# Two cross-attentions of a perceiver: value products ahead of the next value projection, and the V copies behind three row maxima

## The chip, the cores and the metric

The kernel runs on one core of one Trainium2 chip. The metric is the time of a whole execution on the device in microseconds (us); lower is better. Engines are named as in the profile: PE is TensorE (PEld are its weight loads), DVE is VectorE, ACT is ScalarE, POOL is GpSimd and SP issues transfers.

## The reference

Six sublayers are added one after the other to a stream x of 16 sequences of 64 tokens and 256 features. Two of them, the first and the fourth, are cross-attentions to one context of 1601 rows for each sequence, with 16 heads of 16 features:

```
x = x + L0_xattn(layernorm(x), ctx)          # q k v, relative positions, softmax, Wo
x = x + L0_attn(layernorm(x))                # causal, latent keys and values
x = x + L0_ffn(layernorm(x))                 # 8 experts, top 2, and a shared one
x = x + L1_xattn(layernorm(x), ctx, mask)
x = x + L1_attn(layernorm(x))                # gated delta rule and a feed forward
x = x + L1_ffn(layernorm(x))                 # fp4 weights and activations

scores = einsum('bhid,bhjd->bhij', q, k) * scale
out    = einsum('bhij,bhjd->bhid', softmax(scores), v)
```

The first cross-attention also has a table of relative positions (`rel` in the code), the second a mask (`mask`). All tensors are float32.

## The kernel before, in words

Both cross-attentions are made by one function, once with `rel` and once with `mask`. Each goes over the 16 sequences (`b`, in the code `2 * i + p`) in five sections with a loop in the middle. While sequence `b` is attended, the keys and the row maxima of sequence `b + 1` are prepared; that holds for `b` from 0 to 14, so for 15 sequences in each cross-attention. Sequence 15 has nothing to prepare (`ahead` is false).

The 1601 keys lie in 13 chunks of 128 (the last has 65 keys). The loop over `c = 0, 2, ... 12` takes two chunks at a time. In it PE runs four kinds of work:

- `scores(c)`: the negated row maxima are spread over the banks (line 831) and the scores of two chunks added (line 839). ACT then takes their exponential into `PT` (lines 527 and 529).
- `project_values(c + 2)`: eight 256-column products (line 804) make V of the next two chunks in bank `PJ[0]`. DVE copies them to the tile `V` with `values(c + 2)` (line 652), which also frees the bank. The last chunk has half of it.
- `attend_values(c - 2)` and `(c - 1)`: `PT` times `V` of the two chunks before (line 821), 64 small products.
- `maximum(u)`: one of 16 units of the row maxima of the next sequence. PE writes bf16 scores into the banks 5 and 6 (line 779, and line 784 too in units 0 to 3 of the first cross-attention), and DVE reduces them (line 634) to `mx`. There is one pair of banks, so the matmuls of unit `u` wait until DVE has reduced unit `u - 1` (`max_read`). The first unit of a block of keys, u = 4, 8 and 12, has a second wait, for the bf16 keys.

Three tables say where the units stand: `SCORED` behind the scores, `PROJECTED` behind the value projection, `VALUED` behind the value products. In this text a unit that stands behind scores is called S, behind a projection P, behind value products V, with its number: S1, P2, V3, and so on. The tables of before give P0, then S1 P2 V3, S4 P5 V6, S7 P8 V9, S10 P11 V12, S13 P14 V15. No scheduler is at work: each engine runs in the order of the code, and waits only on semaphores. DVE has the same tables and runs in its loop `maximum(SCORED)`, `values(c + 2)`, `maximum(PROJECTED)`, `maximum(VALUED)`. The loop of `c = 12` holds no unit. Behind it DVE reduces `mx` once more to `nm` (line 676).

Of the kernel before, what the change touches and what calls it, by code (L numbers as in the profile page):

```python
# [179 lines left out]
def cross_attention(nc, g, n, m, ctx_t, w, coming, x=None, rel=None, mask=None):  # L180
# [5 lines left out]
    with nc.cleanup_on_exit(), ExitStack() as ctx:  # L186
# [139 lines left out]
            return (Bank(base, stride, i - 1) if 0 < i < B // 2 - 1 else Bank(base)), plans[p], i, p  # L326

        SCORED = {2: 1, 4: 4, 6: 7, 8: 10, 10: 13}
        PROJECTED = {0: 0, 2: 2, 4: 5, 6: 8, 8: 11, 10: 14}
        VALUED = {2: 3, 4: 6, 6: 9, 8: 12, 10: 15}  # L330
        H0 = [0, 1, 4, 5]

        def later(b, k=1):
# [218 lines left out]
        def _(dve):  # L552
# [31 lines left out]
            def body(bank, plan, i, p, flags):  # L584
                ahead, attend, tail = flags
# [74 lines left out]
                for c in range(0, NCH, 2) if attend else ():  # L660
                    if ahead and c in SCORED:
                        maximum(SCORED[c])
                    if c + 2 < NCH:
                        values(c + 2)
                    if ahead and c in PROJECTED:
                        maximum(PROJECTED[c])
                    if ahead and c in VALUED:
                        maximum(VALUED[c])
                if ahead:
                    for u in range(UN) if not attend else ():  # L670
                        maximum(u)
# [23 lines left out]
        def _(pe):  # L695
# [61 lines left out]
            def body(bank, plan, i, p, flags):  # L757
                ahead, attend, tail = flags
# [110 lines left out]
                if attend:  # L869
                    pe.wait_ge(nm_done, b + 1)  # L870
                    pb = take(bank, plan.NM)
                    for r in range(RT):
                        last = pe.matmul(PJ[pb][rows(r), 0:128], nm[:, r, :], g.ident[:, :], start=True, stop=True)
                    last.then_inc(full[pb], 1)
                    if ahead and b:
                        key_block(bank, plan, i, p, NKB - 1)
                    if plan.WO:
                        output()
                    project_values(0)
                    pb, use = plan.NM  # L880
                    pe.wait_ge(free[pb], bank.value(pb, use))
                    if rel:
                        pe.wait_ge(dx_done, b + 1)
                    for c in range(0, NCH, 2):
                        scores(c)
                        if ahead and c in SCORED:
                            maximum(SCORED[c])
                        if c + 2 < NCH:
                            project_values(c + 2)
                        if ahead and c in PROJECTED:  # L890
                            maximum(PROJECTED[c])
                        for a in (c - 2, c - 1) if c else ():
                            attend_values(a)
                        if ahead and c in VALUED:
                            maximum(VALUED[c])
                    follows = next_keys(b)
                    if follows:
                        pe.wait_ge(max_read, UN * (b + 2))
                        key_block(*follows, 0)
                    attend_values(NCH - 1)  # L900
                    if rel:
                        pe.wait_ge(e_done, RD * (b + 1))
                        for j in range(RD):
                            for r in range(4):
                                ej = Ej[:, j, :].rearrange("p (k r q) -> p r k q", r=4, q=S)[:, r]
                                last = pe.matmul(OT[32 * r:32 * r + 32, 0:4 * S], rdv[:, j, :], ej,
                                                 start=False, stop=j == RD - 1, skip_group_check=True)
                        last.then_inc(rv_done, 1)
# [1802 lines left out]
```

## Time and profile before

| | |
|---|---|
| median of 3 runs | 2829.75 us (2828.48 to 2829.79) |
| span of the profiled execution, first to last instruction | 2820.9 us |
| PE busy | 2592.8 us, 92% |
| PE weight loads busy | 1855.1 us, 66% |
| DVE busy | 1386.3 us, 49% |
| ACT busy | 1042.5 us, 37% |
| POOL busy | 532.0 us, 19% |

The profiled execution comes with its span alone, without a time of its own; the span lies 8.9 us under the median of the runs. An execution on one core has no neighbour, so the page is that of the only core. Busy shares are means over very different stages: the cross-attentions fill about the stretches 70 to 880 us and 1320 to 2050 us.

### The profile page before, as it was taken

How to read it: one execution, taken by the hardware profiler on the slowest of the kernel's cores; microseconds unless marked ns; L12 is line 12 of the kernel's file. 1: busy time of each engine (PE TensorE's matmuls, PEld its weight loads, DVE VectorE, ACT ScalarE, POOL GpSimd, SP SyncE). 2: the span in 40 equal slices, each digit the busy share in tenths (PEclk: the TensorE clock that was granted, in tenths of full speed). 3: DMA queues.
4: the chain of work that ended last, by engine and by line, in shares of the span. 5: the costliest groups of instructions: out<-in, count | busy, mean ns of one | idle time of the engine just before them, and what ended most of it. 6: DMA issues, size and time to landing. Idle time of an engine off the chain costs nothing. (4 is left out here: it accounts for less than half of the span.)

```text
span 2820.9 us, 91874 instructions
## 1 busy us (share of the span) xinstructions
PE 2592.8 (92%) x42047; PEld 1855.1 (66%) x42047; DVE 1386.3 (49%) x2238; ACT 1042.5 (37%) x1400; POOL 532.0 (19%) x400
## 2 busy tenths in 40 slices
PE   7999999999999789998999999999979999988798
PEld 3666666666666556664666666666647777777466
DVE  4454544544544831115545455555465454554378
ACT  2333333333323421114444444444434445444223
POOL 2423424434324000002111111111011111111000
PEclk8999999999998579999999999999999999999899
DMA  2110110110100030101111111112010000000200
GB/s 90 32 43 25 37 37 25 37 37 27 42 20 2 1 121 30 45 20 44 43 33 41 34 40 37 37 37 68 3 51 3 3 3 3 4 3 4 79 1 16
DMA packets 49607, 88.88 MB, mean 32 GB/s; under 512 B 8544, under 2 KB 44224, under 8 KB 47952
## 3 DMA queue, kind: packets, MB, share of 16 engines
q1 hardware_dynamic: 49200, 83.08, 9.6%
q8 instruction: 331, 5.42, 0.8%
q14 instruction: 44, 0.36, 0.0%
q0 software_dynamic: 32, 0.02, 0.0%
HBM read 82.04 MB, written 1.05 MB: 29 GB/s over the span
## 5 line engine op out<-in xcount | busy, mean ns | idle before, releaser
L634 DVE TENSOR_REDUCE x_mx<-banks 128x2 f32<-128x800 f32 (+1 forms) x512 | 505.3, 990 | 162.4 <-PE banks L779 133.2
L804 PE MATMUL banks<-x_wv,x_cT 128*128 128x256 f32 (+1 forms) x1664 | 419.3, 394 | 12.3 <-DVE x_nmb L641 12.3
L709 PE MATMUL banks<-x_cT,x_wk 128*128 128x400 f32 (+1 forms) x1024 | 385.4, 519 | 9.3 <-DMA x_cT<-in_ctx 5.9
L804 PEld LDWEIGHTS banks<-x_wv,x_cT 128*128 128x128 f32 (+1 forms) x1664 | 296.4, 187 | 83.6 <-issue 24.5
L527 ACT ACTIVATE x_PT<-banks 128x2048 f32<-128x2048 f32 (+1 forms) x112 | 196.5, 1755 | 372.1 <-PE banks L839 372.1
L529 ACT ACTIVATE x_PT<-banks,x_kbs 128x1024 f32<-128x1024 f32 (+1 forms) x208 | 221.1, 1110 | 287.7 <-PE banks L839 287.7
L652 DVE COPY x_V<-banks 128x512 f32<-128x512 f32 (+1 forms) x224 | 146.2, 653 | 338.1 <-PE banks L804 337.7
L709 PEld LDWEIGHTS banks<-x_cT,x_wk 128*128 128x128 f32 x1024 | 189.5, 193 | 140.5 <-issue 26.8
L839 PE MATMUL banks<-x_qbd,x_kT 32*128 32x128 f32 x6656 | 248.6, 272 | 0.0
L839 PEld LDWEIGHTS banks<-x_qbd,x_kT 32*128 32x128 f32 x6656 | 244.0, 183 | 3.5
L821 PE MATMUL banks<-x_PT,x_V 128*32 128x64 f32 x13312 | 233.8, 221 | 3.8 <-issue 3.0
L821 PEld LDWEIGHTS banks<-x_PT,x_V 128*32 128x32 f32 x13312 | 196.7, 110 | 55.4 <-issue 47.5
L779 PE MATMUL banks<-x_kbf,x_qbf 32*128 32x400 bf16 (+1 forms) x1024 | 174.8, 339 | 53.5 <-DVE x_mx L634 44.9
L406 POOL TENSOR_TENSOR x_kbf<-x_kT,x_mb 128x802 bf16<-128x802 f32 (+1 forms) x64 | 110.2, 1725 | 597.4 <-ACT x_kT L464 597.4
L447 POOL TENSOR_TENSOR x_Ej<-x_PT,x_kmask 128x1024 f32<-128x1024 f32 x64 | 148.7, 2358 | 128.8 <-ACT x_PT L527 128.8
L779 PEld LDWEIGHTS banks<-x_kbf,x_qbf 32*128 32x128 bf16 x1024 | 49.7, 91 | 176.2 <-DVE x_mx L634 91.8
L2069 PE MATMUL banks<-d_KQ,d_KB 64*64 64x64 f32 x3584 | 129.3, 221 | 7.4 <-ACT d_KB L1743 3.5
L1415 DVE SCALAR_TENSOR_TENSOR X<-banks,e_comb,X 128x256 f32<-128x256 f32 x72 | 34.8, 484 | 205.5 <-PE banks L1453 205.5
L464 ACT ACTIVATE x_kT<-banks,x_bk 128x400 f32<-128x400 f32 (+1 forms) x128 | 76.0, 594 | 158.6 <-PE banks L709 158.6
L2069 PEld LDWEIGHTS banks<-d_KQ,d_KB 64*64 64x64 f32 x3584 | 117.1, 134 | 23.2 <-issue 23.0
L1440 PE MATMUL banks<-XNT,e_wu 128*128 128x512 f32 x288 | 128.6, 600 | 0.4 <-DVE e_pr L1366 0.4
L1453 PE MATMUL banks<-e_wd,e_hT 128*128 128x256 f32 x576 | 127.1, 379 | 0.0
(353 smaller groups left out, 3671.4 us busy)
## 6 DMA issues: line engine op xcount, KB each, us to landing
x_cT<-in_ctx SPq DMA_DIRECT2D x96, 400.0 KB, 3.6
x_cT<-in_ctx SPq DMA_DIRECT2D x32, 401.0 KB, 3.6
e_wu<-in_mo_up SPq DMA_DIRECT2D x9, 512.0 KB, 3.5
e_wd<-in_mo_down SPq DMA_DIRECT2D x9, 512.0 KB, 4.5
x_mrow<-in_mask_row SPq DMA_DIRECT2D x1, 3202.0 KB, 16.2
t_w<-in_db_w SPq DMA_DIRECT2D x3, 1024.0 KB, 7.2
d_wqk<-in_db_qk SPq DMA_DIRECT2D x1, 2048.0 KB, 7.9
t_wgu<-in_fp_gu SPq DMA_DIRECT2D x1, 1536.0 KB, 10.4
```

Source lines behind the costliest of these rows:

```text
L447: pool.tensor_tensor(Ej[:, j, :].rearrange("p (h q) -> p h q", h=H), PT[:, 0, 0, :].rearrange("p (h q) -> p h q", h=H), kmask[:, j, None, ...
L527: act.activation(out, got, ACT.Exp, scale=HD ** -0.5, bias=0.0).then_inc(exp_done, n2)
L529: act.activation(out[:, :, a], got[:, :, a], ACT.Exp, scale=HD ** -0.5, bias=kbs[0:CHK[c], p, c + a:c + a + 1]).then_inc(exp_done, 1)
L634: dve.reduce_max(mx[:, H0[k]:H0[k] + 3:2, kb], g.PS[:, first:first + 2, 0:KBS[kb]], AXX).then_inc(max_read, 1)
L652: dve.tensor_copy(V[0:CHK[c], c % 6:c % 6 + n2, :, 0:HD], PJ[pb][0:CHK[c], 0:D * n2].rearrange("p (a h d) -> p a h d", a=n2, h=H)).then_in ...
L709: last = pe.matmul(PJ[pb][:, 0:KBS[k]], wk[:, c, gg, :], cT[:, (p + 1) % 2, c, KB0[k]:KB0[k] + KBS[k]], start=c == 0, stop=c == KC - 1)
L779: last = pe.matmul(g.P[first + x][:, 0:KBS[kb]], qbf[rows(r), gg, :, :].rearrange("p i q -> p (i q)"), kbf[rows(r), gg, keys], start=True, ...
L804: last = pe.matmul(PJ[pb][0:CHK[c + k], D * k:D * k + D], cT[:, p, cc, 128 * (c + k):128 * (c + k) + CHK[c + k]], wv[:, cc, :], start=cc = ...
L821: last = pe.matmul(OT[r:r + 32, S * (h // 4):S * (h // 4) + S], V[0:CHK[c], c % 6, h, :], PT[0:CHK[c], c // 2 % NPT, c % 2, S * h:S * h + ...
L839: last = pe.matmul(SC[r][0:CHK[c + a], at:at + HPT * S], kT[rows(r), p, gg, 128 * (c + a):128 * (c + a) + CHK[c + a]], qbd[rows(r), p, gg, ...
L1440: last = pe.matmul(g.P[f][:, :], wu[:, q, c, 128 * f:128 * f + 128], g.XNT[:, c, 512 * t:512 * t + 512], start=c == 0, stop=c == KC - 1)
L2069: last = pe.matmul(out, lhs(E[e], hp), rhs(E[e], hp), start=k > 0 or start, stop=True, skip_group_check=True)
```

## The change

Three edits go together. On PE the value products of chunks `c - 2` and `c - 1` stand directly behind the scores' unit, ahead of the projection of `c + 2`. The tables swap their numbers, so that units still run in the order 0 to 15: P0, then S1 V2 P3, S4 V5 P6, S7 V8 P9, S10 V11 P12, S13 V14 P15. On DVE the copy `values(c + 2)` stands behind all three maxima of its turn, no longer behind the first. No instruction is added or removed.

```diff
         SCORED = {2: 1, 4: 4, 6: 7, 8: 10, 10: 13}
-        PROJECTED = {0: 0, 2: 2, 4: 5, 6: 8, 8: 11, 10: 14}
-        VALUED = {2: 3, 4: 6, 6: 9, 8: 12, 10: 15}
+        VALUED = {2: 2, 4: 5, 6: 8, 8: 11, 10: 14}
+        PROJECTED = {0: 0, 2: 3, 4: 6, 6: 9, 8: 12, 10: 15}
...
                     if ahead and c in SCORED:
                         maximum(SCORED[c])
+                    if ahead and c in VALUED:
+                        maximum(VALUED[c])
+                    if ahead and c in PROJECTED:
+                        maximum(PROJECTED[c])
                     if c + 2 < NCH:
                         values(c + 2)
-                    if ahead and c in PROJECTED:
-                        maximum(PROJECTED[c])
-                    if ahead and c in VALUED:
-                        maximum(VALUED[c])
...
                         scores(c)
                         if ahead and c in SCORED:
                             maximum(SCORED[c])
+                        for a in (c - 2, c - 1) if c else ():
+                            attend_values(a)
+                        if ahead and c in VALUED:
+                            maximum(VALUED[c])
                         if c + 2 < NCH:
                             project_values(c + 2)
                         if ahead and c in PROJECTED:
                             maximum(PROJECTED[c])
-                        for a in (c - 2, c - 1) if c else ():
-                            attend_values(a)
-                        if ahead and c in VALUED:
-                            maximum(VALUED[c])
```

PE in the first cross-attention, the turns c = 8 and c = 10 of a sequence. Before, with the scores of c = 8 (lines 831 and 839) first:

```order
L831 MATMUL banks<-x_nmb,x_ones 128x512 x4
L839 MATMUL banks<-x_qbd,x_kT 128x128 x16
L779 MATMUL banks<-x_kbf,x_qbf 128x400 x2
L804 MATMUL banks<-x_wv,x_cT 128x256 x4
L779 MATMUL banks<-x_kbf,x_qbf 128x400 x2
L821 MATMUL banks<-x_PT,x_V 32x64 x32
L779 MATMUL banks<-x_kbf,x_qbf 128x400 x2
L831 MATMUL banks<-x_nmb,x_ones 128x512 x4
L839 MATMUL banks<-x_qbd,x_kT 128x128 x16
```

And in the changed kernel at the same place:

```order
L831 MATMUL banks<-x_nmb,x_ones 128x512 x4
L839 MATMUL banks<-x_qbd,x_kT 128x128 x16
L779 MATMUL banks<-x_kbf,x_qbf 128x400 x2
L821 MATMUL banks<-x_PT,x_V 32x64 x32
L779 MATMUL banks<-x_kbf,x_qbf 128x400 x2
L804 MATMUL banks<-x_wv,x_cT 128x256 x4
L779 MATMUL banks<-x_kbf,x_qbf 128x400 x2
L831 MATMUL banks<-x_nmb,x_ones 128x512 x4
L839 MATMUL banks<-x_qbd,x_kT 128x128 x16
```

The value products (line 821) moved ahead of the projection (line 804); a unit (line 779) stands behind each block as before, and each block still has a unit on both sides. (A matmul of float32 counts once here and twice in the profile.)

DVE at the end of a sequence of the first cross-attention, the last copies (line 652), maxima (line 634) and the last reduction (line 676). Before:

```order
L634 TENSOR_REDUCE x_mx<-banks 128x2 x3
L652 COPY x_V<-banks 128x32x16
L634 TENSOR_REDUCE x_mx<-banks 128x2 x3
L652 COPY x_V<-banks 65x16x16
L634 TENSOR_REDUCE x_mx<-banks 128x2 x2
L676 TENSOR_REDUCE x_nm<-x_mx 128x4x2
```

And in the changed kernel:

```order
L634 TENSOR_REDUCE x_mx<-banks 128x2 x3
L652 COPY x_V<-banks 128x32x16
L634 TENSOR_REDUCE x_mx<-banks 128x2 x3
L652 COPY x_V<-banks 65x16x16
L676 TENSOR_REDUCE x_nm<-x_mx 128x4x2
```

In the first listing a copy stands between the maxima S and P of a turn (the groups of three are P, V, S), in the second between P and the next S (S, V, P). The copy of 65 rows has moved from behind S13 to behind P15.

## Rows read from the trace of the kernel before

**Rows 1.** The page, first line.

```profile
span 2820.9 us, 91874 instructions
```

**Rows 2.** Busy time by stretch (length, PE, PEld, DVE, ACT, POOL, PEclk, DMA), both cross-attentions.

```profile
88.00:816.00 728.00, 704.81 (x11974) 499.32 (x11962) 357.63 (x442) 243.94 (x224) 265.95 (x180) 1.00 0.12 34
1352.00:2007.00 655.00, 626.22 (x10950) 439.23 (x10948) 333.67 (x428) 285.21 (x322) 94.27 (x56) 1.00 0.14 39
```

**Rows 3.** Waits over the whole span: total us, times, longest.

```profile
PEld banks L779 <- DVE x_mx L634: 91.8, 278, 0.6
...
PE banks L779 <- DVE x_mx L634: 44.9, 120, 0.5
```

**Rows 4.** Timeline, first cross-attention, P8 to V15 (start, duration, engine, line).

```profile
300.63 0.34 PE L779 MATMUL banks<-x_kbf,x_qbf 32*128 32x400 bf16 x2
300.74 0.69 DVE L652 COPY x_V<-banks 128x512 f32<-128x512 f32 x1 [0.93 <-PE banks L804]
...
301.35 0.98 DVE L634 TENSOR_REDUCE x_mx<-banks 128x2 f32<-128x800 f32 x1
...
302.39 0.34 PE L779 MATMUL banks<-x_kbf,x_qbf 32*128 32x400 bf16 x2 [0.38 <-DVE x_mx L634]
...
302.77 0.99 DVE L634 TENSOR_REDUCE x_mx<-banks 128x2 f32<-128x800 f32 x1 [0.44 <-PE banks L779]
...
303.82 0.34 PE L779 MATMUL banks<-x_kbf,x_qbf 32*128 32x400 bf16 x2
...
306.02 0.34 PE L779 MATMUL banks<-x_kbf,x_qbf 32*128 32x400 bf16 x2
...
307.86 0.34 PE L779 MATMUL banks<-x_kbf,x_qbf 32*128 32x400 bf16 x2 [0.47 <-DVE x_mx L634]
...
309.29 0.34 PE L779 MATMUL banks<-x_kbf,x_qbf 32*128 32x400 bf16 x2
...
310.73 0.34 PE L779 MATMUL banks<-x_kbf,x_qbf 32*128 32x400 bf16 x2
...
312.16 0.34 PE L779 MATMUL banks<-x_kbf,x_qbf 32*128 32x400 bf16 x2
```

**Rows 5.** Timeline, last sequence of the first cross-attention: value products, then scores.

```profile
865.80 1.10 PE L821 MATMUL banks<-x_PT,x_V 128*32 128x64 f32 x64
866.83 0.40 PE L831 MATMUL banks<-x_nmb,x_ones 32*128 32x512 bf16 x4
```

**Rows 6.** Timeline of DVE behind the last maximum of a sequence.

```profile
313.57 0.19 DVE L676 TENSOR_REDUCE x_nm<-x_mx 128x8 f32<-128x32 f32 x1
313.68 0.41 DVE L598 TENSOR_TENSOR x_qbd<-x_qT,x_hmt 128x256 f32<-128x256 f32 x1
```

**Rows 7.** Timeline, first cross-attention: P0, S1, its maximum, P2, V3, S4.

```profile
285.48 0.34 PE L779 MATMUL banks<-x_kbf,x_qbf 32*128 32x401 bf16 x2
...
287.23 0.34 PE L779 MATMUL banks<-x_kbf,x_qbf 32*128 32x401 bf16 x2
...
287.84 0.99 DVE L634 TENSOR_REDUCE x_mx<-banks 128x2 f32<-128x802 f32 x1 [0.67 <-PE banks L784]
...
289.54 0.34 PE L779 MATMUL banks<-x_kbf,x_qbf 32*128 32x401 bf16 x2
...
291.30 0.34 PE L779 MATMUL banks<-x_kbf,x_qbf 32*128 32x401 bf16 x2 [0.15 <-DVE x_mx L634]
...
293.05 0.34 PE L779 MATMUL banks<-x_kbf,x_qbf 32*128 32x400 bf16 x2
```

**Rows 8.** Timeline, second cross-attention: P0, the scores of c = 2, S1.

```profile
1559.73 0.34 PE L779 MATMUL banks<-x_kbf,x_qbf 32*128 32x401 bf16 x2
...
1560.20 0.10 PEld L831 LDWEIGHTS banks<-x_nmb,x_ones 32*128 32x128 bf16 x4 [0.38 <-ACT x_PT L529]
...
1561.48 0.34 PE L779 MATMUL banks<-x_kbf,x_qbf 32*128 32x401 bf16 x2
```

## The prediction

> **What bounds the kernel now.** I read the table by stretch first, then the waits, then the timeline of single turns. In both cross-attentions PE is busy for 704.8 of 728 us and 626.2 of 655 us, DVE for about half, and the granted clock is 1.00, the upper of the two levels (2.4 GHz) [rows 2]. So PE sets the pace there, and only two things can shorten it: less work or fewer waits. The table of waits shows one wait that comes back in every turn: a unit of maxima (line 779) waits for the reduction of the unit before (line 634), 91.8 us on the side of the weight loads, 44.9 us on the side of the matmuls [rows 3]. That is the most that a change of order among these can win; all other work of PE stays.
>
> The timeline shows where that wait sits. Starts of units follow at 1.76 (P8 to V9), 1.43 (V9 to S10), 2.20 (S10 to P11), 1.84 (P11 to V12), and at the end 1.43 (V12 to S13), 1.44 (S13 to P14) and 1.43 us (P14 to V15) [rows 4]. The 2.20 us holds a whole projection and waits for nothing. The 1.43 us is the least distance that one pair of banks allows: a reduction starts 0.38 us behind its unit (302.77 behind 302.39), takes 0.99 us, and 0.06 us later the next unit starts. The stretch with the value products in it is longer than both of its contents: 0.27 us from unit to products and 1.03 us of products (865.80 to 866.83) [rows 5] would be 1.30 us. It is 1.76 us because the reduction of P8 starts at 301.35, 0.72 us behind its unit and not 0.38: DVE first copies the V that the projection has just left (300.74, start to next start 0.61 us) [rows 4]. PE runs its shortest block under DVE's longest turn. V12 costs 0.09 us more, as it has a second wait (keys of a new block), which shows only where the unit is held by `max_read`.
>
> **The change part by part.** Work: the same instructions, the same banks, no transfer moved (SP waits for scores alone). Each block of PE keeps a unit before and behind it, so there are no more switches between tile shapes. What changes is the distance between units, so I work out each turn by two rules: a unit starts when PE has done the block before, and not before the reduction of the last unit is over plus 0.06 us; a reduction starts 0.38 us behind its unit, or when DVE is free.
>
> *The new seam.* The copy now follows the reduction of P. No row shows this pair back to back with the copy ready. Bounds: independent neighbours on DVE overlap by 0.08 us both in copy to reduction (0.61 us for a copy of 0.69) [rows 4] and in the reduction of line 676 to its neighbour with a wait long satisfied (0.11 us for one of 0.19) [rows 6]; then the copy starts 0.91 us behind the reduction. Without this overlap it is 1.00 us. I take 0.91, as the nearer pair by kind is a reduction followed by another operation. Then the copy starts at P + 1.29 us and the next reduction can start at P + 1.90 us.
>
> *Steady turns (small units).* P to S lies across scores and stays 1.43 us (they fit, as behind V now). S's reduction would start at P + 1.81 and starts at P + 1.90, 0.09 us later, so V follows S by 1.43 + 0.09 = 1.52 us. PE needs only 1.30 us for that stretch. V8 now is the unit with the second wait that is held: 1.61 us. V to P holds the projection: 2.20 us as before. P12's second wait lies under it and costs nothing.
>
> *First cross-attention.* Units 0 to 3 are long (line 784 too), their reduction starts 0.61 us behind (287.84) [rows 7], with room for the copy behind P0. S1 to V2: 0.61 + 0.99 + 0.05 = 1.65 us, where P2 to V3 was 1.76 us [rows 7]. P3 to S4 is 1.75 us as V3 to S4 [rows 7]; the copy behind P3 is over at 0.61 + 0.91 + 0.61 = 2.13 us, just when S4's reduction wants to start (1.75 + 0.38), so S4 to V5 is 1.43 us. P0 to S1 gains nothing: scores fill it.
>
> | stretch over the value products | V3, now V2 | V6, V5 | V9, V8 | V12, V11 | V15, V14 | sum |
> |---|---|---|---|---|---|---|
> | before, both | 1.76 | 1.76 | 1.76 | 1.84 | 1.43 | 8.55 |
> | after, first | 1.65 | 1.43 | 1.61 | 1.52 | 1.52 | 7.73 |
> | after, second | 1.43 | 1.43 | 1.61 | 1.52 | 1.52 | 7.51 |
>
> The last column of units is a loss of 0.09 us: behind the short projection there was no copy in the way, and now the copy of P12 is. S13's other neighbour, 1.44 us over the short projection, stays.
>
> *Second cross-attention.* Unit 0 is short, so S1's reduction (1.75 + 0.38 us behind P0) meets a free DVE: 1.43 us. S4 has the second wait and comes 0.09 us later, which clears the copy. P0 to S1 is held by ACT, not by DVE alone: the scores of c = 2 wait for the exponential until 1560.20, and S1 follows 1.28 us behind [rows 8], about the length of the scores. I count no gain there.
>
> *Edits at nothing.* The copy of c + 2 comes about 1 us later in its turn. PE needs it twice: the bank for the projection of c + 4 and the products of c + 2. The copy ends at P + 1.98 us; the next projection starts at 1.43 + 1.52 + 0.27 = P + 3.22 us, so 1.2 us of cover. The products come a turn later still. The last, short copy stands ahead of the reduction to `nm` and delays it by some 0.35 us; PE wants `nm` only behind two blocks of keys. Sequence 15 has no units; its three blocks only change places.
>
> **Sum.** First: 8.55 - 7.73 = 0.82 us a sequence. Second: 8.55 - 7.51 = 1.04 us. Fifteen sequences each: 15 x 1.86 = 27.9 us, within the 44.9 to 91.8 us of this wait. Against its own profile the span goes from 2820.9 [rows 1] to 2793.0 us; the median of the runs lies 8.9 us above the span, so 2829.75 becomes 2801.9 us.
>
> **The rivals.**
> - *The copy doesn't start under the reduction.* At 1.00 us from start to start every held S-to-V is 0.09 us longer, four a sequence, 10.8 us in all (4 x 0.09 x 30): 2813 us. If nothing on DVE overlapped at all (0.99 + 0.69 us) the copy would hold S's reduction to P + 2.06 us, 0.16 us more on three units and 0.15 on V5: about 19 us of the gain gone, 2821 us. For it: the pair isn't in the trace; against it: rows 4 and 6 overlap. Chance 0.15 together. By the Trainium skill, "VectorE: DVE Perf Modes", section "The DRAIN you can't avoid", the next operation doesn't start until the pipeline is empty; by that rule it would be the second of these times. The 0.61 us of the copy speaks against it here.
> - *The copy hides wholly.* V8, V11 and V14 at the least distance: 3 x 0.09 x 30 = 8.1 us more, 2794 us. For it: the timeline's modelled starts are uncertain by hundredths. Chance 0.06.
> - *No change.* PE's gain is taken back at the end of each sequence, where something else (exponentials, transfers, POOL) sets the pace: within 5.7 us of before. Against it: PE is the busy engine at 96%, ACT and POOL below half [rows 2]. Chance 0.07.
> - *Slower: the projection waits for its bank.* The copy frees `PJ[0]` behind three reductions. If it came more than 1.2 us later than I place it, each of some 150 projections would wait, and 28 / 150 = 0.19 us beyond the cover the gain would be gone; a copy 1.5 us late costs 0.3 x 150 = 45 us, 2847 us. I see nothing that delays the copy so far, as P's reduction starts 0.38 us behind its unit. Chance 0.04.
> - *The time of what follows.* Later stages start 12 us earlier or more (15 x 0.82), and the clock there changes level in steps; I allow a few us either way, in the range.
>
> **How the numbers follow.** The forecast has 0.68, own range 2796 to 2808. A measurement tells no change from one under 0.2%, 5.7 us. The first rival lies at 2813 to 2821 and counts as faster, so faster is 0.68 + 0.15 + 0.06 = 0.89, same 0.07, slower 0.04. The range takes in the hidden copy below and the nearer half of the first rival above: 2793 to 2815 us.
>
> **What would show it.** In the profile after: the wait of line 779 for line 634 falls by about 28 us of its 91.8; DVE shows reductions in threes with the copy 0.91 us behind the start of the third; S-to-V distances of 1.43 to 1.65 us, V-to-P 2.20, P-to-S unchanged; no wait of line 804 for line 652. The forecast is wrong if the copy-to-reduction seam is longer, if line 804 waits for its bank, or if the value products behind S take more than 1.52 us of PE.

## The result and the profile after

The change makes the kernel faster, by more than was forecast. Beside the kernel before on one chip it took 2785.67 us (2784.48 to 2788.49, 4 runs) against 2829.77 us (2828.48 to 2829.99, 4 runs): ratio 0.9853, 95% interval 0.9838 to 0.9868. In three later sets the changed kernel stood at 2785.71, 2784.40 and 2787.15 us, but the kernel before at 2821.45, 2821.40 and 2824.62 us, ratios 0.9873, 0.9869 and 0.9869 (intervals from 0.9853 to 0.9890). So the change is worth about 37 us, and the first comparison shows 44.1 us. The forecast was 2801.9 us, a gain of 27.9 us, with a range from 2793 to 2815.

The page of the changed kernel:

```profile
span 2782.0 us, 91874 instructions
...
PE 2588.3 (93%) x42047; PEld 1856.8 (67%) x42047; DVE 1370.1 (49%) x2238; ACT 1043.6 (38%) x1400; POOL 533.0 (19%) x400
```

The span was 2820.9 us [rows 1]; the numbers of instructions are the same. The waits for the reduction, to be held against [rows 3] (total us, times, longest):

```profile
PEld banks L779 <- DVE x_mx L634: 67.4, 254, 0.6
```

The row of line 779 from the table of lines (count | busy, mean ns | idle before, releasers):

```profile
L779 PE MATMUL banks<-x_kbf,x_qbf 32*128 32x400 bf16 (+1 forms) x1024 | 173.7, 337 | 23.9 <-DVE x_mx L634 6.4 <-POOL x_Dxb L433 3.0
```

The waits for line 634 fell from 91.8 to 67.4 us on the side of the weight loads, and from 44.9 to 6.4 us on the side of the matmuls.

The timeline of the first cross-attention, from P6 to V11, answers to [rows 4] (start, duration, engine, line):

```profile
283.41 0.34 PE L779 MATMUL banks<-x_kbf,x_qbf 32*128 32x400 bf16 x2
...
283.79 0.99 DVE L634 TENSOR_REDUCE x_mx<-banks 128x2 f32<-128x800 f32 x1 [1.21 <-PE banks L779]
...
284.70 0.68 DVE L652 COPY x_V<-banks 128x512 f32<-128x512 f32 x1
...
284.84 0.34 PE L779 MATMUL banks<-x_kbf,x_qbf 32*128 32x400 bf16 x2
...
285.11 1.10 PE L821 MATMUL banks<-x_PT,x_V 128*32 128x64 f32 x64
285.30 0.98 DVE L634 TENSOR_REDUCE x_mx<-banks 128x2 f32<-128x800 f32 x1
...
286.42 0.34 PE L779 MATMUL banks<-x_kbf,x_qbf 32*128 32x400 bf16 x2 [0.21 <-DVE x_mx L634]
...
288.63 0.34 PE L779 MATMUL banks<-x_kbf,x_qbf 32*128 32x400 bf16 x2
...
290.06 0.34 PE L779 MATMUL banks<-x_kbf,x_qbf 32*128 32x400 bf16 x2
...
291.56 0.34 PE L779 MATMUL banks<-x_kbf,x_qbf 32*128 32x400 bf16 x2
```

The copy starts 0.91 us behind the start of P6's reduction (284.70 behind 283.79), as taken, and the next reduction 0.60 us behind the copy. S7 to V8 is 1.58 us, S10 to V11 1.50, V8 to P9 2.21, P6 to S7 and P9 to S10 1.43 us. DVE is idle for 1.21 us ahead of P6's reduction: it now has its slack in front of P, under the projection. Before, the copy stood there and delayed the reduction that PE waits for.

The start of a sequence in the second cross-attention, P0, the scores of c = 2, S1, V2, against [rows 8]:

```profile
1528.06 0.34 PE L779 MATMUL banks<-x_kbf,x_qbf 32*128 32x401 bf16 x2
...
1528.54 0.10 PEld L831 LDWEIGHTS banks<-x_nmb,x_ones 32*128 32x128 bf16 x4 [0.39 <-ACT x_PT L529]
...
1529.66 0.33 PE L779 MATMUL banks<-x_kbf,x_qbf 32*128 32x401 bf16 x2
...
1531.09 0.34 PE L779 MATMUL banks<-x_kbf,x_qbf 32*128 32x401 bf16 x2
```

The scores wait for the exponential as before (1528.54 - 1528.06 = 0.48 us; it was 0.47), but S1 follows the scores 1.12 us later and no longer 1.28 us. P0 to S1 is 1.60 us, not 1.75.

From P0 to the last unit a sequence now takes 25.72 us in the first and 25.09 us in the second cross-attention; it took 26.68 and 26.35 us (measured between the starts of units in fourteen sequences of each, all within 0.02 us). The first sequence of each gained 0.87 and 1.10 us. Together: 0.87 + 14 x 0.96 + 1.10 + 14 x 1.26 = 33.1 us.

That leaves some 4 us of the 37. They lie between sequences: the key projection of the next sequence starts late there. In three of fifteen sequences of each cross-attention of the kernel before, PE stops inside the value products of chunks 10 and 11:

```profile
208.19 0.98 PE L821 MATMUL banks<-x_PT,x_V 128*32 128x64 f32 x53
210.06 0.41 PE L821 MATMUL banks<-x_PT,x_V 128*32 128x64 f32 x11 [0.89 <-issue]
210.40 0.94 PE L709 MATMUL banks<-x_cT,x_wk 128*128 128x401 f32 x2
```

Of 64 matmuls 53 run, then PE stands for 0.89 us without a semaphore ("issue"), then come the other 11. The table of waits of before counts six such stops ahead of matmuls:

```profile
PE banks L821 <- issue: 3.0, 6, 0.9
```

The 3.0 us understate them, as the idle time counts from the modelled end of the matmul in front, 0.22 us behind its start. Between the starts of the 53rd and the 54th matmul lie 1.11 us, where two neighbours are else at most 0.06 us apart. In these six sequences the key projection starts 1.18, 0.53, 0.88, 0.39, 1.07 and 0.41 us later than in the others, 4.5 us in all. At the same place the changed kernel has

```profile
197.27 1.10 PE L821 MATMUL banks<-x_PT,x_V 128*32 128x64 f32 x64
198.30 0.94 PE L709 MATMUL banks<-x_cT,x_wk 128*128 128x401 f32 x2
```

and no such row in its table of waits.

The profiles show the same without the time of the whole execution. From the first unit of a cross-attention's 15 sequences to the last one, the kernel before takes 755.3 and 682.5 us, the changed one 738.3 and 661.8 us: 17.0 and 20.7 us less, 37.7 us together. The four profiles of the changed kernel agree in the sum of the two stretches to 0.4 us, the two of the kernel before to 0.5 us.

### The profile page after: what moved, and what is told of

Same layout as the page of the kernel before. It is cut to its first block and busy times, and to the rows that moved or that the text cites. A ratio compares the mean times of both kernels' runs of the same rounds, so it can differ in the third digit from the quotient of the medians.

```text
span 2782.0 us, 91874 instructions
## 1 busy us (share of the span) xinstructions
PE 2588.3 (93%) x42047; PEld 1856.8 (67%) x42047; DVE 1370.1 (49%) x2238; ACT 1043.6 (38%) x1400; POOL 533.0 (19%) x400
## 3 DMA queue, kind: packets, MB, share of 16 engines
q8 instruction: 331, 5.42, 0.8%
## 5 line engine op out<-in xcount | busy, mean ns | idle before, releaser
L804 PEld LDWEIGHTS banks<-x_wv,x_cT 128*128 128x128 f32 (+1 forms) x1664 | 297.5, 188 | 83.6 <-issue 24.4
L821 PE MATMUL banks<-x_PT,x_V 128*32 128x64 f32 x13312 | 232.2, 221 | 0.8 <-ACT x_PT L529 0.5
L821 PEld LDWEIGHTS banks<-x_PT,x_V 128*32 128x32 f32 x13312 | 196.1, 110 | 50.7 <-issue 47.3
```

What stands on the lines that cost most here:

```text
L804: last = pe.matmul(PJ[pb][0:CHK[c + k], D * k:D * k + D], cT[:, p, cc, 128 * (c + k):128 * (c + k) + CHK[c + k]], wv[:, cc, :], start=cc = ...
L821: last = pe.matmul(OT[r:r + 32, S * (h // 4):S * (h // 4) + S], V[0:CHK[c], c % 6, h, :], PT[0:CHK[c], c // 2 % NPT, c % 2, S * h:S * h + ...
```

## The experiments

In all of them the sums named are from the start of P0 to the start of unit 15, and ratios are against the kernel before in the same set. The absolute times that the expectations of e3 and e4 name start from the first set's 2829.8 us; the kernel before stood at 2819.88 us in theirs.

The table gives, for every profile, both cross-attentions from their first unit to their last, added up. It leaves out the stages in front of, between and behind them, where most of the spread between executions lies.

| profile | both cross-attentions, us |
|---|---|
| before; e1 | 1437.81; 1438.29 |
| changed kernel; e5; e9; e15 | 1400.15; 1400.51; 1400.19; 1400.27 |
| e2, PE's order of before, copy behind P | 1409.0 |
| e3, PE's order of before, copy last | 1435.4 |
| e4, changed order, copy ahead of P | 1433.6 |
| e6, first alone; e7, second alone | 1421.0; 1418.3 |
| e8; e10, copies on ACT | 1400.8; 1401.0 |
| e11, copy in halves | 1407.1 |
| e12, e13, one turn exchanged | 1433.1; 1407.7 |
| e14, copies on ACT and changed order | 1394.7 |

**e1: the kernel before again.**

> The kernel before, unchanged, profiled and timed once more. The distances between the units account for 33.4 us of the gain (15 x 0.94 in the first cross-attention, 15 x 1.29 less what b = 0 has of its own in the second), the medians show 44.1 us. Theory A: the rest is the clock: in the profile after the change PE reaches the first query products at 24.1 us and not 27.9, ahead of any changed instruction, so the half clock of the first 90 us falls otherwise from execution to execution. Then this profile differs from the first one by 3 us or more in the span, with the distances between units unchanged to 0.02 us. Theory B: the kernel before always has that prologue, and this profile has its span within 1 us of 2820.9 and its first query products at 27.9 us.

2819.2 us (2809.26 to 2822.29, 12 runs), before 2819.88 us (2809.06 to 2824.47, 29 runs): ratio 0.9997 (0.9984 to 1.0010). Distances as in the first profile (26.68 and 26.34 us), the six stops too. The span, 2819.6 us, is 1.3 us off the first, which is neither of the two bounds named; the first query products come at 25.7 us and not 27.9, so the start does move from one execution to the next. The main yield is the spread: the kernel before runs anywhere from 2809 to 2824 us on this chip; the two profiles of it have the same distances in the cross-attentions. e1 alone decides between neither theory; e5 does.

**e2: PE's order as before, copy behind P.**

```diff
                     if ahead and c in SCORED:
                         maximum(SCORED[c])
-                    if c + 2 < NCH:
-                        values(c + 2)
                     if ahead and c in PROJECTED:
                         maximum(PROJECTED[c])
+                    if c + 2 < NCH:
+                        values(c + 2)
                     if ahead and c in VALUED:
                         maximum(VALUED[c])
```

> PE's order and the tables as before the change; on DVE the V copy of a turn stands behind the maximum P and ahead of V. Theory A (the place of the copy behind the reduction of P is all that pays): P to V is 1.43 us and not 1.76, V to S grows from 1.43 to 1.50, nothing else changes; sums from P0 to unit 15: 25.63 us in the first and 25.08 in the second cross-attention, so within 2 us of the changed kernel, about 2785 us. Theory B (PE's new order is needed): the time stays near that of before, over 2815 us.

2788.78 us (4 runs), ratio 0.9890 (0.9875 to 0.9905). P to V is 1.43 us, V to S 1.50 us. The sums are 25.88 and 25.27 us, 0.25 and 0.19 us above what was expected: S1 to P2 grew from 2.31 to 2.52 and from 2.20 to 2.37 us, since at c = 0 the copy stands behind P0 and the projection of c = 4 waits for its bank (line 804 for line 652, 6.3 us on the weight loads' side). The six stops are there too, 4.1 us in the gaps. Theory A in the main. Most of the gain comes from the copy's place behind the reduction of P alone: 15 x (0.80 + 1.08) = 28 us.

**e3: PE's order as before, copy last.**

```diff
                     if ahead and c in SCORED:
                         maximum(SCORED[c])
-                    if c + 2 < NCH:
-                        values(c + 2)
                     if ahead and c in PROJECTED:
                         maximum(PROJECTED[c])
                     if ahead and c in VALUED:
                         maximum(VALUED[c])
+                    if c + 2 < NCH:
+                        values(c + 2)
```

> PE's order and the tables as before the change; on DVE the V copy stands behind all three maxima of its turn, which now end with V. Theory A (this order needs PE's new one for its bank): the copy ends 2.0 us behind V, and the next projection wants its bank 1.7 us behind V; line 804 waits 0.2 to 0.32 us in each turn for line 652, which eats the 0.33 us that P to V gains; 2829 us within 5. Theory B (the bank is free in time): 25.6 and 25.1 us from P0 to unit 15, about 2785 us.

2816.96 us (12 runs), ratio 0.9987 (0.9975 to 1.0000). Theory A. The bank is late in each turn (the copy, the weight loads and matmuls of line 804, and the total from the table of waits):

```profile
299.38 0.68 DVE L652 COPY x_V<-banks 128x512 f32<-128x512 f32 x1
...
300.12 1.59 PEld L804 LDWEIGHTS banks<-x_wv,x_cT 128*128 128x128 f32 x8 [0.50 <-DVE x_V L652]
300.12 1.99 PE L804 MATMUL banks<-x_wv,x_cT 128*128 128x256 f32 x8 [0.25 <-DVE x_V L652]
```

```profile
PEld banks L804 <- DVE x_V L652: 63.7, 134, 0.5
```

P to V fell to 1.43 us and S to P rose to 2.52 (2.43 once, 2.36 in the second for S1 to P2); the sums are 26.79 and 26.12 us. This is the mechanism of the prediction's slower rival at work: a copy that stands last needs PE's new order, which puts the value products and a unit ahead of the projection.

**e4: PE's order as changed, copy ahead of P.**

```diff
                     if ahead and c in VALUED:
                         maximum(VALUED[c])
-                    if ahead and c in PROJECTED:
-                        maximum(PROJECTED[c])
                     if c + 2 < NCH:
                         values(c + 2)
+                    if ahead and c in PROJECTED:
+                        maximum(PROJECTED[c])
```

> PE's order and tables as changed; on DVE the V copy stands directly behind its projection, ahead of the maximum P, as it stood before the change. Theory A (PE's order alone moves the wait and removes none): S to V falls to 1.43 us, P to S rises to 1.76 us, the sums are 26.66 and 26.33 us as before the change, the time 2830 within 5 us. Theory B (PE's order itself pays, as the products fill the time of a reduction): a gain of 10 us or more over before.

2813.29 us (12 runs), ratio 0.9975 (0.9963 to 0.9986). The distances are as theory A says: S to V 1.43, P to S 1.75 us (a held unit with a second wait 0.09 us more, V2 of the first 1.66), sums 26.69 and 26.36 us. P's reduction waits out the copy:

```profile
305.02 0.34 PE L779 MATMUL banks<-x_kbf,x_qbf 32*128 32x400 bf16 x2
...
305.12 0.69 DVE L652 COPY x_V<-banks 128x512 f32<-128x512 f32 x1 [0.93 <-PE banks L804]
...
305.73 0.98 DVE L634 TENSOR_REDUCE x_mx<-banks 128x2 f32<-128x800 f32 x1
...
306.77 0.34 PE L779 MATMUL banks<-x_kbf,x_qbf 32*128 32x400 bf16 x2 [0.30 <-DVE x_mx L634]
```

Yet it is 6.6 us faster than before, and neither theory had that: with equal sums inside the sequences, the gaps between them hold no stop, which is worth 4.5 us. The rest of the 6.6 is within the spread of the executions. This gap led to the stop shown above.

**e5, e6, e7: the change again, and in one cross-attention alone.** e6 and e7 keep both orders in the code and choose; e7 has `NEW = rel is None`.

```diff
+        NEW = rel is not None
+        PROJECTED = {0: 0, 2: 3, 4: 6, 6: 9, 8: 12, 10: 15} if NEW else {0: 0, 2: 2, 4: 5, 6: 8, 8: 11, 10: 14}
+        VALUED = {2: 2, 4: 5, 6: 8, 8: 11, 10: 14} if NEW else {2: 3, 4: 6, 6: 9, 8: 12, 10: 15}
```

> The changed kernel, unchanged, timed beside the kernel before on one chip. Theory A (the change is worth what the distances between units show, 15 x 0.94 + 15 x 1.26 and 0.4 to 1 us of the first turns, about 33.5 us; the 44.1 us of the first comparison held some 10 us of the executions of before, whose half-clock stretches vary): ratio 0.988, within 0.002. Theory B (a further 10 us comes with the change, outside the cross-attentions' turns): ratio 0.9845.

> The change in the first cross-attention alone (tables, PE's order and DVE's order), the second as before. Theory A (each stage pays by its own distances): 15 x 0.94 = 14 us, ratio 0.995. Theory B (a hidden gain behind the first stage): over 20 us, ratio under 0.993.

> The change in the second cross-attention alone. Theory A: 15 x 1.26 = 19 us and up to 1 us of the first sequence, ratio 0.993. Theory B: another share than the distances give, over 25 or under 14 us.

e5: 2785.71 us (4 runs) against 2821.45 (11 runs), ratio 0.9873 (0.9856 to 0.9890), 35.7 us. e6: 2806.45 us (6 runs), 0.9946 (0.9927 to 0.9964), 15.0 us. e7: 2801.19 us (6 runs), 0.9935 (0.9918 to 0.9952), 20.3 us. Each stage has its new distances only where it is changed (25.73 and 26.35 us in e6, 26.69 and 25.10 us in e7), and the stops are gone there alone: 14.3 us and some 2.5 of stops, 18.7 us and some 2. The two parts (15.0 and 20.3 us) make up the whole (35.7 us), so nothing of size hides elsewhere. The interval of e5 holds theory A's 0.988 and not theory B's 0.9845; A's 33.5 us left out the stops.

**e8, e10: the V copies on ACT, PE's order as before.** `values(c)` moves from DVE's stream to ACT's, behind the exponentials of the turn, as an activation with Copy; DVE keeps the maxima.

```diff
+                    act.activation(V[0:CHK[c], c % 6:c % 6 + n2, :, 0:HD],
+                                   PJ[pb][0:CHK[c], 0:D * n2].rearrange("p (a h d) -> p a h d", a=n2, h=H),
+                                   ACT.Copy).then_inc(free[pb], 1)
...
                         for a in range(n2) if mask else ():
                             act.activation(out[:, :, a], got[:, :, a], ACT.Exp, scale=HD ** -0.5,
                                            bias=kbs[0:CHK[c], p, c + a:c + a + 1]).then_inc(exp_done, 1)
+                        if c + 2 < NCH:
+                            values(c + 2)
```

> PE's order and tables as before the change; the V copies are made by ACT behind the exponentials of the turn, and DVE has the maxima alone. Theory A (the copy on DVE was the whole wait): every held distance is the least one, 1.43 us (1.51 at unit 12), sums from P0 to unit 15 of 25.5 us in the first and 24.9 us in the second cross-attention against 25.71 and 25.09 of the changed kernel, so some 6 us faster than that, ratio to before 0.986. Theory B (ACT becomes late: the copy takes longer there or pushes the exponentials, and PE waits at the scores or the projection): slower than the changed kernel, ratio over 0.990.

> The copies on ACT once more beside the changed kernel. Its distances between units are shorter by 0.2 us in each sequence of either cross-attention, 6 us in all. Theory A (the time follows the distances): 6 us under the changed kernel of the same set. Theory B (what the medians showed, about 1 us): the 6 us go into later stages, whose half-clock stretches shift.

The distances are the least ones throughout, sums 25.54 and 24.90 us. In the set of e8 and e5 the time went down by 1 us where 5.6 us were to come, in the set of e10 and e9 it went up by 2.5: 2784.75 us, ratio 0.9871 (0.9854 to 0.9889), and again 2786.93 us, 0.9883 (0.9867 to 0.9899), where the changed kernel had 2785.71 and 2784.40. The six stops are there, longer than before:

```profile
PE banks L821 <- issue: 4.6, 6, 1.1
```

In the gaps between sequences they cost 6.1 us (4.5 in the kernel before), in e8 and in e10 alike. The shorter distances gave 5.6 us and the stops took 6.1: both cross-attentions together are 0.3 to 0.8 us longer than in the changed kernel of the same set (1400.8 and 1401.0 us). So theory B of e10 looked in the wrong place: the gain is lost inside the cross-attentions, not in later stages.

**e9, e15: the changed kernel a third and a fourth time.**

> The changed kernel a third time, for the size of the change in another set of executions of before. Theory A (the change is worth 33.5 us; the kernel before varies by some 10 us from set to set, the changed one by less): the changed kernel at 2785.5 to 2788 us, the ratio between 0.985 and 0.990. Theory B (the first comparison was the true size): ratio 0.9853 within 0.001.

> The changed kernel beside e14 on the same chip: 2785 us within 2, no stall between sequences.

Ratios 0.9869 (0.9853 to 0.9886) and 0.9869 (0.9853 to 0.9884), the time 2784.40 and 2787.15 us, no stop in either profile. The interval of e9 reaches into theory B's range too, so its time doesn't decide. Its profile has the two cross-attentions at 1400.2 us, as the first had: the change is worth the same there each time, 37.7 us, and the rest of the first 44.1 lies outside them.

**e11: each V copy in two halves.**

```diff
-                    dve.tensor_copy(V[0:CHK[c], c % 6:c % 6 + n2, :, 0:HD],
-                                    PJ[pb][0:CHK[c], 0:D * n2].rearrange("p (a h d) -> p a h d", a=n2, h=H)).then_inc(free[pb], 1)
+                    for k in range(n2):
+                        last = dve.tensor_copy(V[0:CHK[c + k], c % 6 + k:c % 6 + k + 1, :, 0:HD],
+                                               PJ[pb][0:CHK[c + k], D * k:D * k + D].rearrange("p (a h d) -> p a h d", a=1, h=H))
+                    last.then_inc(free[pb], 1)
```

> The changed kernel with each V copy made as two copies of one chunk. A copy of 256 columns took 0.41 us alone, so the pair is some 0.08 us longer to the next start than the one of 0.68 us. Theory A (behind P the copy holds the reduction of S and with it V): S7 to V8, S10 to V11 and S13 to V14 grow by 0.08 us, V2 and V5 stay or grow by less, P to S and V to P don't change; 7 us slower at most. Theory B (the distance S to V of 1.50 is PE's own, value products): no distance changes.

The pair takes 0.74 us (from 300.27, the next reduction starts at 300.93: 0.66 us where the one copy has 0.60), the sums grew by 0.23 us each, to 25.95 and 25.32: three held distances by 0.06 to 0.07 us, S4 to V5 by 0.04. Theory A: S to V hangs on the copy. The time, 2795.69 us (4 runs, ratio 0.9906, 0.9889 to 0.9922), is 11.3 us over the changed kernel of its set, where the distances give 15 x 0.46 = 7 us. Against the profile of e9, with a span 11.8 us shorter, the cross-attentions of e11 take 6.9 us more; the other 4.9 us lie in stages that the edit doesn't touch (2.7 us in front of the first unit, 2.6 behind the last).

**e12, e13: one turn alone.** e12 is the kernel before with the turn c = 10 in the changed order, e13 the changed kernel with c = 10 in the old one (each with its units 14 and 15 exchanged in the tables, and DVE's order to match). The cut shows PE's new branch in e12.

```diff
+                        if c == 10:
+                            for a in (c - 2, c - 1) if c else ():
+                                attend_values(a)
+                            if ahead and c in VALUED:
+                                maximum(VALUED[c])
+                            if c + 2 < NCH:
+                                project_values(c + 2)
+                            if ahead and c in PROJECTED:
+                                maximum(PROJECTED[c])
```

> The kernel before with the turn c = 10 alone in the changed order on PE (value products of chunks 8 and 9, V14, the short projection, P15); DVE keeps its copies directly behind the projections. The distances between units stay as before (26.68 and 26.35 us from P0 to unit 15). Theory A (the stall of PE inside the value products of chunks 10 and 11, 0.4 to 1.4 us in three of fifteen sequences of either cross-attention, comes from two blocks of value products that stand close together with no projection between them): the stall is gone, the gaps between sequences are 24.25 or 25.98 and 19.44 or 21.17 us alone, 4.5 us less than before. Theory B (it comes from the place of the other blocks or of the copies): the gaps of 25.4, 24.8 and 26.9 us stay, the time is that of before.

> The changed kernel with the turn c = 10 alone in the order of before (short projection, P14, value products of 8 and 9, V15). The short projection then wants its bank 1.70 us behind P12, and the copy behind P12 ends at about 2.0 us, so S13 to P14 is about 1.70 us, and P0 to unit 15 some 0.2 us longer than 25.72 and 25.09: 6 us. Theory A (two close blocks of value products make the stall): 4.5 us come on top in the gaps of three sequences each, 10 us in all over the changed kernel. Theory B: the gaps stay clean, 6 us in all.

e12: 2818.30 us (12 runs) against 2824.81 (17 runs), ratio 0.9973 (0.9964 to 0.9983). The distances are those of before (26.68 and 26.34 us); all gaps are 24.25 or 25.98, and 19.44 or 21.17 us. The value products of chunks 10 and 11 run through:

```profile
200.06 1.10 PE L823 MATMUL banks<-x_PT,x_V 128*32 128x64 f32 x64
201.09 2.96 PE L711 MATMUL banks<-x_cT,x_wk 128*128 128x401 f32 x8
```

e13: 2793.95 us (4 runs), ratio 0.9891 (0.9875 to 0.9907), and the stop is back:

```profile
201.30 1.10 PE L823 MATMUL banks<-x_PT,x_V 128*32 128x64 f32 x64
...
203.28 0.97 PE L823 MATMUL banks<-x_PT,x_V 128*32 128x64 f32 x53
204.89 0.41 PE L823 MATMUL banks<-x_PT,x_V 128*32 128x64 f32 x11 [0.63 <-issue]
```

In the old order the two blocks of 64 matmuls start 1.98 us apart, with the short last scores between them; in the new one a projection lies between them as well, and they start 3.41 us apart in e12. The sums grew less than expected (25.83 and 25.19 us: S13 to P14 became 1.60 us, the wait for the bank 0.25), and the stops of the gaps add 4.3 us: with 3.2 us of distances, 7.5 us more in the cross-attentions than in the changed kernel. Theory A in both. So the order of the turn c = 10 makes the stops and removes them.

What PE waits for there, no experiment varied by itself, but the traces hold more on it. The list of DMA queues of before has one that loads instructions (packets, MB, share of 16 engines):

```profile
q8 instruction: 331, 5.42, 0.8%
```

331 packets are 5.42 MB, 16 KB each, for some 85,800 records of PE in the trace, so a packet holds some 256 instructions. Counted along PE's records in order of their starts, the three stops of each cross-attention lie whole multiples of 256 apart: 27 x 256 and 34 x 256 in the first, twice 31 x 256 in the second. They come before the same matmul in every profile that has them (number 54, 42 and 63 of the 64 in the first, 50, 50 and 41 in the second); only their lengths differ.

Cutting PE's records of both cross-attentions at these places and at all others a multiple of 256 away gives some 180 stretches of 256 in each profile. Ahead of all 48 stops PE went through its 256 instructions in 2.53 to 2.59 us. No other stretch in any of the 17 profiles took less than 3.57 us, and none of them ended in such a stop; in the changed kernel the six stretches in question take 3.9 to 4.0 us. PE stands 1.06 to 2.18 us behind the start of the last instruction packet and goes on 2.15 to 2.85 us behind it. So the stop reads as PE being through with its loaded instructions before the next packet is usable, and in the other sequences the fast pair of blocks is cut by the end of a packet. e12 and e13 moved the stop by thinning out the stretch and packing it again; no run changed the loading itself.

**e14: the copies on ACT and PE's changed order.** PE's order of the change as well, and over e8:

```diff
-        PROJECTED = {0: 0, 2: 2, 4: 5, 6: 8, 8: 11, 10: 14}
-        VALUED = {2: 3, 4: 6, 6: 9, 8: 12, 10: 15}
+        VALUED = {2: 2, 4: 5, 6: 8, 8: 11, 10: 14}
+        PROJECTED = {0: 0, 2: 3, 4: 6, 6: 9, 8: 12, 10: 15}
```

> The changed order on PE and the changed tables, with the V copies on ACT behind the exponentials. Theory A (the copy on DVE and the stall are two separate costs): distances of 25.5 us in the first (e8) and 24.9 us in the second cross-attention, no stall between sequences, so 6 us under the changed kernel. Theory B (ACT is late: it copies later in the turn, and in the second cross-attention also makes the mask row at c = 4): PE waits for exponentials or the bank, no faster than the changed kernel.

2780.77 us (2778.00 to 2783.34, 5 runs), ratio 0.9842 (0.9829 to 0.9855), against 2787.15 us of the changed kernel in the same set: 6.4 us less, where 15 x 0.37 = 5.6 us was to come. Theory A. Sums 25.54 and 24.90 us, no stop. ACT copies under PE's work and makes nobody wait; the copy of 65 rows as an example, and the least distance of two units behind it (301.09 to the reduction at 301.47, as after any unit):

```profile
301.04 0.38 ACT L513 ACTIVATE x_V<-banks 65x256 f32<-65x256 f32 x1 [0.76 <-PE banks L804]
...
301.09 0.34 PE L779 MATMUL banks<-x_kbf,x_qbf 32*128 32x400 bf16 x2
301.47 0.99 DVE L647 TENSOR_REDUCE x_mx<-banks 128x2 f32<-128x800 f32 x1 [0.44 <-PE banks L779]
```

It is the fastest version here.

## Why the prediction was right or wrong

*What bounds the kernel.* Right. PE sets the pace, and its waits for the reduction were the thing to win. But the list of what PE could win was short by one entry: "only two things can shorten it: less work or fewer waits" left out stops without a semaphore. The row `PE banks L821 <- issue` was in the same table of waits.

*The distances.* The two rules, applied to P-to-S, S-to-V and V-to-P, hold to 0.03 us. S1 to V2 1.66 (forecast 1.65) in the first and 1.43 in the second, S4 to V5 1.43 in both, S7 to V8 1.58 (1.61), S10 to V11 and S13 to V14 1.50 (1.52). The seam that no row had shown is 0.91 us, so the rival of a copy that doesn't start under the reduction is out, and with it the second of its times. For that one the prediction cited the Trainium skill, "VectorE: DVE Perf Modes", section "The DRAIN you can't avoid", and read half of it: the same paragraph adds that a next operation that is not held starts earlier. The trace agrees with that: 0.91 us from start to start with a reduction of 0.99. The few hundredths of difference made 15 x 0.12 = 1.8 us more.

*Where a term was wrong: P0 to S1.* "P0 to S1 gains nothing: scores fill it" and "I count no gain there" were mistaken. The first cross-attention went from 1.75 to 1.66 us, the second from 1.75 to 1.60. The prediction took 1.28 us [rows 8] for about the length of the scores (in the first cross-attention the same stretch was 1.25 us), but the end of these stretches was held by the reduction of P0, which itself stood behind a copy; the scores alone are 1.12 to 1.16 us. The prediction's own rule had it: a reduction 0.71 us behind P0 holds S1 to 0.71 + 0.98 + 0.06 = 1.75 us, the distance in the trace. The timeline of before showed the holder (second cross-attention, P0 at 1559.73):

```profile
1560.44 0.98 DVE L634 TENSOR_REDUCE x_mx<-banks 128x2 f32<-128x802 f32 x1
...
1561.48 0.10 PEld L779 LDWEIGHTS banks<-x_kbf,x_qbf 32*128 32x128 bf16 x2 [0.18 <-DVE x_mx L634]
```

In the runs, e1 and e4 (copy ahead of P0's reduction) have 1.75 us, e2, e3, e8 and the changed kernel (copy behind it or not on DVE) have 1.59 to 1.66 us. Worth 15 x 0.24 = 3.6 us.

*What was missing: the stop.* PE's new order was costed at nothing but a change of places. It removes six stops of PE, 4.5 us, which e12 shows by itself (ratio 0.9973, with the distances unchanged), e4 too, and e13 brings back.

*The sum.* 27.9 us forecast. The distances gave 33.1: 27.9, with 3.6 of P0 to S1 and 1.8 of the hundredths on top, less 0.2 as the first sequences gained less. With 4.5 us of stops that makes 37.6 us, and the cross-attentions of the two profiles differ by 37.7. The later sets show 35.7 to 37.5 us. The sign that the prediction named, the waits of the weight loads down by about 28 us, came out at 24.4 (91.8 to 67.4); that of the matmuls fell by 38.5.

*The base.* "The median of the runs lies 8.9 us above the span" was used as a constant and isn't one. Later executions lie 2 to 3 us above their spans (2784.48 and 2782.0 us for the changed kernel, 2821.4 and 2819.6 in e1). By that, the profile of before was of a faster execution than the three beside it, whose 2829.75 us stand at the high end of what this kernel does (2809 to 2833 us over the sets). This made the miss larger: from the 2821 to 2825 us of the later sets, the same 27.9 us would have given 2793.5 to 2796.7 us, still 8 to 10 us above what was measured. The profiles differ in stages that nobody touched: in the first 88 us PE had a granted clock of 0.88 in the mean, in the changed kernel's first 83 us 0.98; in the gated-delta stages the reverse:

```profile
0.00:88.00 88.00, 69.72 (x486) 40.26 (x488) 37.04 (x71) 22.39 (x30) 32.83 (x31) 0.88 0.25 77
2080.00:2643.00 563.00, 490.44 (x13392) 401.48 (x13392) 277.55 (x551) 259.45 (x449) 83.31 (x96) 0.98 0.02 3
```

```profile
0.00:83.00 83.00, 66.69 (x592) 40.12 (x592) 39.44 (x73) 23.76 (x31) 32.87 (x31) 0.98 0.26 83
2035.00:2603.00 568.00, 495.24 (x13392) 405.49 (x13392) 277.10 (x549) 260.12 (x449) 83.54 (x96) 0.97 0.01 3
```

(First of before, then of after: length, PE, PEld, DVE, ACT, POOL, PEclk, DMA.) The same PE instructions take 563 us in one and 568 in the other. From profile to profile the first unit comes at 68 to 76 us, and what follows the last unit takes 808 to 822 us. Why the first set of before ran 5 to 10 us above the later ones is not settled; its slower executions weren't profiled.

*The rivals.* No change: excluded, no interval of the changed kernel comes near 1. The projection that waits for its bank: not here, but real, at 0.25 us a turn where PE's order isn't changed along (e3). The copy that hides wholly came true only on ACT (e14).

So the step that failed is the list of gains on PE. P0 to S1 was put at nothing and gave 3.6 us; PE's new order was put at nothing beyond the distances and removed 4.5 us of stops. Both had rows in the trace of before. The mechanism that was forecast, the copy behind P's reduction, was right.

## What to carry to other kernels

Where one pair of banks ties two engines together, put the second engine's other work behind the reduction whose successor on the first engine is longest anyway, and work out each distance with two rules and their numbers; here it came out to 0.03 us. A distance whose end is held by the other engine says nothing about the length of the work inside it: look for the same work in a place where nothing waits. Read "issue" rows on the pacing engine as well as semaphore waits, and compare equal sequences with each other: one that is longer than its twins shows a stop. Where PE issues hundreds of small matmuls in a row, count its instructions too: putting other work between two blocks of them cost nothing here and removed the stops.

## What the runs showed of the hardware

- PE stopped for 0.2 to 1.4 us without a semaphore, after 40 to 62 of 64 small matmuls, in three of fifteen sequences, when two blocks of 64 matmuls, each with its weight loads, started 1.98 us apart; with a projection in between as well (the changed kernel, e12: 3.4 us apart and more) it never did. The twelve other sequences had the 1.98 us too and no stop. It hits the same sequences, before the same matmul, in each profile. The pairs follow at 16 ns (64 in 1.03 us), so such a block goes through 128 instructions in 1 us.
- The queue that loads instructions moves packets of 16 KB, one for some 256 of PE's (331 packets for 85,800). The stops lie whole multiples of 256 instructions apart. After 256 instructions in 2.53 to 2.59 us PE stopped each time (48 of 48), after 3.57 us or more never (some 3,000 stretches). That PE runs out of loaded instructions fits all of it; no run varied the loading.
- On DVE a copy started 0.08 us before the reduction in front of it ended, with both of its semaphores long satisfied: two waits cost nothing there. On PE a second wait of a held unit cost 0.08 to 0.09 us (1.58 against 1.50, 1.52 against 1.43 in e14).
- The executions of one kernel spread over 15 us (2809 to 2824 in the set of e1), while the distances inside the cross-attentions were equal to 0.02 us in all profiles of one kernel. The granted clock in front of the cross-attentions differed (0.88 and 0.98 in the two profiles shown). For a change of a few us the distances tell more than the time.
